# Last attention, first pass: one row maximum per bank of 500 columns instead of one over both banks

## The chip, the cores and the metric

One core of a Trainium2 chip runs the whole network in one launch. The metric is the device time of a launch in microseconds (us), the median of several runs. The engines of the core that matter here are PE (TensorE, matmul), DVE (VectorE), ACT (ScalarE), POOL (GpSimd) and SP (SyncE, which issues transfers). They run their own instruction streams in order and meet only at semaphores.

## What is computed

The network has four rounds of cross attention and feed-forward over 32 batches of 56 tokens; the keys and values come from a context of 1500 rows for each batch. The change lies in the last attention, cut here to what matters:

```python
def _L3_xattn_ref(query, key_value, Wq, bq, Wk, bk, Wv, bv, Wo, bo):
    NUM_HEADS = 16
    CLAMP = 10000.0
    ...
    scale = D ** (-0.5)
    q = (query @ Wq + bq).reshape(B, Nq, H, D).transpose(0, 2, 1, 3)
    k = (key_value @ Wk + bk).reshape(B, Nkv, H, D).transpose(0, 2, 1, 3)
    v = (key_value @ Wv + bv).reshape(B, Nkv, H, D).transpose(0, 2, 1, 3)
    attn = jnp.einsum('bhqd,bhkd->bhqk', q, k) * scale
    attn = jnp.clip(attn, -CLAMP, CLAMP)
    attn = jax.nn.softmax(attn, axis=-1)
    ...
    x = jnp.einsum('bhqk,bhkd->bqhd', attn, v).reshape(B, Nq, Cq)
    return x @ Wo + bo
```

With B = 32, Nq = 56, Nkv = 1500, 16 heads of 8 values. The softmax needs the maximum over the 1500 keys of each query and head before the exponential.

## The kernel before, in words

The function `clipped_pass` computes this attention in two passes over the scores of a batch. The first pass finds the maxima: with queries on the partitions (two heads of 56 queries, 112 rows) and keys on the free axis, 24 matmuls of 500 columns (eight pairs of heads, three thirds of the keys) are made two at a time. Such a pair of matmuls, each into a PSUM bank of its own, is a chunk; a batch has 12 chunks. `chunks` (PE) makes a chunk, `chunk_max` (DVE) takes the maximum of both banks in one reduction of 112 x 1000 elements to two columns of `mp`. After the twelfth, two small DVE instructions finish the eight maxima of the batch (`mu`, `mc`), POOL splits them into bf16 parts, and PE turns them.

The second pass makes the scores again, with keys on the partitions: 12 tiles of 125 keys, each 896 wide. For each tile PE scores it (`score`, 8 matmuls), DVE clips it out of PSUM (`clip_tile`), ACT takes the exponential, and PE multiplies it with the values (`weigh`, 16 small matmuls).

The two passes of different batches run interleaved. In slot k of batch b, PE makes in this order: the scores of tile k+2, the weighing of tile k, one chunk of the first pass of batch b+1 or b+2, and at last a piece of other work in the fifth bank (`fifth_bank`: the keys of batch b+3 in slots 0 to 2, the turning of the maxima, the sums, the values of the next batch in slots 7 to 10). DVE makes in the same slot: the clip of tile k+2, then the maximum of the chunk. The order is written out by hand; nothing is scheduled at run time.

Of the eight PSUM banks, 0 to 3 hold two score tiles, 4 the weighed sums, 5 the other work, and 6 and 7 the chunk (`CB[0]`). So the chunk has one buffer: PE's next chunk waits (`chunk_maxed`) until DVE's reduction of the last is done. Only the first 21 chunks, made before the second pass has begun, rotate over three pairs of banks (`CB[n % 3]`); the 363 chunks behind them (384 less 21) use banks 6 and 7 alone.

The keys made in the fifth bank are copied out by ACT twice (line 2119 as bf16, line 2123 in full), and PE's next keys wait for the second copy. In ACT's stream these two copies stand behind an exponential.

Of the kernel before, what the change touches and what calls it, by code (L numbers as in the profile page):

```python
# [19 lines left out]
ALU = mybir.AluOpType  # L20
ACT = mybir.ActivationFunctionType
AX = mybir.AxisListType
# [6 lines left out]
TT = 112  # L29
# [1598 lines left out]
def clipped_pass(core, L, S, src, bo, scale, clip, csum, ctx, norm):  # L1628

    nc, d, ps = core.nc, core.d, core.ps  # L1630

    def sb(n, shape, dt=F32, c=ctx):
        return core.sb(f"{L}_{n}", shape, dt, c)
# [13 lines left out]
    mp, mu, mc = sb("mp", [TT, 24]), sb("mu", [TT, 8]), sb("mc", [TT, 8])  # L1647
# [9 lines left out]
    CB = [slice(6, 8), slice(0, 2), slice(2, 4)]  # L1657
# [81 lines left out]
    first = Eight(None, 0)  # L1739
# [48 lines left out]
    with nc.Block() as block:  # L1788
        @block.sync
        def _(sp):  # L1790
            def place_part(b, n):
                sp.wait_ge((S["keys_first"], S["keys_second"], S["keys_third"])[n], b.lin(3, 3))
                for u, (part, _) in enumerate(PRODUCTS):
                    if part == n:
                        sp.dma_start(KS[b.r % 4][u:NPROD * PF:NPROD, 0:PAIRS * NK], key_part(b, part)[:, :]
                                     ).then_inc(S[f"keys_in{b.r % 4}"], 16)

            def place_keys(b):
                if b.turn is not None or b.r >= 4:
                    sp.wait_ge(S["scored"], b.lin(12, -36))  # L1800
                sp.wait_ge(S["keys_third"], b.lin(3, 3))
                for u, (part, _) in enumerate(PRODUCTS):
                    sp.dma_start(KS[b.r % 4][u:NPROD * PF:NPROD, 0:PAIRS * NK], key_part(b, part)[:, :]
                                 ).then_inc(S[f"keys_in{b.r % 4}"], 16)
# [122 lines left out]
        def _(pe):  # L1927
            def make_keys(b, c):
                if c == 0:
                    pe.wait_ge(S["ck_in"], b.lin(16, 16))  # L1930
                nc.tensor.matmul(key_bank(b, c), WK[:, :], CK[:, columns(c)], start=True, stop=True
                                 ).then_inc(S["keys_made"], 1)
# [59 lines left out]
            def chunks(b, c, pair=0):  # L1992

                if c == 0:
                    pe.wait_ge(S[f"keys_in{b.r % 4}"], uses(b, 4, 96))
                    pe.wait_ge(S[f"q_in{b.r % 4}"], uses(b, 4, 192) - (0 if b.r % 4 else 48))
                    if b.r == 0:
                        pe.wait_ge(S["q_first"], 48)
                if pair == 0 and (b.turn is not None or b.r >= 2 or (b.r, c) >= (1, 9)):
                    pe.wait_ge(S["chunk_maxed"], b.lin(12, c))  # L2000
                elif b.r or c >= 3:
                    pe.wait_ge(S["chunk_maxed"], b.lin(12, c - 2))
                for a in range(2):
                    m, p = (2 * c + a) // 3, (2 * c + a) % 3
                    mm = nc.tensor.matmul(ps[:, CB[pair].start + a, 0:500],  # L2005
                                          QS[b.r % 4][0:96, m * 2 * NQ:m * 2 * NQ + 128],
                                          KS[b.r % 4][0:96, m * NK + p * 500:m * NK + (p + 1) * 500],
                                          start=True, stop=True)
                mm.then_inc(S["chunk_scored"], 1)

            def uses(b, every, each):

                if b.turn is None:
                    return (b.r // every + 1) * each
                return (8 // every * each) * b.turn + (b.r // every + 1) * each

            def score(b, n):
                if n == 0:
                    pe.wait_ge(S["keys_zeroed"], min(2 * b.r + 2, 8))
                    pe.wait_ge(S[f"max_in{b.r % 2}"], uses(b, 2, 16))  # L2020
                if b.turn is not None or b.r or n >= 2:
                    pe.wait_ge(S["clipped"], b.lin(12, n - 1))
                for m in range(PAIRS):
                    k0 = m * NK + n * KP
                    mm = nc.tensor.matmul(SB[n % 2][:, m // 4, m % 4 * 2 * NQ:(m % 4 + 1) * 2 * NQ]  # L2025
                                          .rearrange("p (j q) -> p j q", j=2), KS[b.r % 4][:, k0:k0 + 128],
                                          queries(b)[:, m, :, :], start=True, stop=True)
                mm.then_inc(S["scored"], 1)
# [14 lines left out]
            def body(b):  # L2043
                for k in range(KT):
                    if k + 2 < KT:
                        score(b, k + 2)
                    elif (b + 1).there():
                        score(b + 1, k + 2 - KT)
                    weigh(b, k)
                    of, c = chunk_of(b, k)  # L2050
                    if of.there():
                        chunks(of, c)
                    fifth_bank(b, k)
# [28 lines left out]
            for n in range(21):  # L2082
                chunks(first + n // 12, n % 12, n % 3)
                if n == 13:
                    turn(first)
                if n in (16, 18, 20):
                    c = (n - 16) // 2
                    if c:
                        pe.wait_ge(S["keys_copied"], 6 + c)
                    else:  # L2090
                        pe.wait_ge(S["turn_copied"], 1)
                    make_keys(first + 2, c)
            pe.wait_ge(S["chunk_maxed"], 21)
            score(first, 0)
            score(first, 1)
            pe.wait_ge(S["ones_set"], 2)
# [129 lines left out]
        def _(dve):  # L2226
# [11 lines left out]
                         part_columns(P[:, 0:2, :], c))  # L2238
                dve.sem_inc(S["q_split"], 1)

            def chunk_max(b, c, pair=0):
                dve.wait_ge(S["chunk_scored"], b.lin(12, c + 1))
                nc.vector.tensor_reduce(mp[:, 2 * c:2 * c + 2], ps[0:TT, CB[pair], 0:500], AX.X, ALU.max  # L2243
                                        ).then_inc(S["chunk_maxed"], 1)
                if c < 11:
                    return
                dve.wait_ge(S["chunk_maxed"], b.lin(12, 12))
                nc.vector.tensor_reduce(mu[:, :], mp[:, :].rearrange("p (t c) -> p t c", c=3), AX.X, ALU.max
                                        ).then_inc(S["max_found"], 1)
                dve.wait_ge(S["max_found"], b.lin(1, 1))  # L2250
                nc.vector.tensor_scalar(mc[:, :], mu[:, :], clip, -clip, ALU.min, ALU.max
                                        ).then_inc(S["max_ready"], 1)

            def clip_tile(b, n):
                if n == 0:
                    dve.wait_ge(S[f"lb_in{b.r % 2}"], b_uses(b))
                dve.wait_ge(S["scored"], b.lin(12, n + 1))
                if b.turn is not None or b.r or n >= 3:
                    dve.wait_ge(S["weighed"], b.lin(12, n - 2))
                nc.vector.scalar_tensor_tensor(out=two(P[0:KP, n % 3, :]), in0=SB[n % 2][0:KP], scalar=0.0,  # L2260
                                               in1=two(LB[0:KP, b.r % 2, :]), op0=ALU.min, op1=ALU.max
                                               ).then_inc(S["clipped"], 1)
# [13 lines left out]
            def body(b):  # L2276
                for k in range(KT):
                    if k + 2 < KT:
                        clip_tile(b, k + 2)
                    elif (b + 1).there():  # L2280
                        clip_tile(b + 1, k + 2 - KT)
                    of, c = chunk_of(b, k)
                    if of.there():
                        chunk_max(of, c)
                    if b.r % 2 == 0 and (b - 2).there() and k == 3:
                        invert(b - 2)
# [16 lines left out]
            for t in VS:  # L2303
                nc.vector.memset(by_head(t)[:, :, DH:DH + 1], 1.0).then_inc(S["ones_set"], 1)
            for n in range(21):
                chunk_max(first + n // 12, n % 12, n % 3)
            clip_tile(first, 0)
            clip_tile(first, 1)
            batches(dve, body)
# [1508 lines left out]
```

## Time and profile before

| | us |
|---|---|
| median of 3 runs | 4166.52 |
| lowest and highest | 4165.03, 4169.4 |
| the profiled execution, device time | 4166.84 |
| its span in the trace | 4165.2 |
| of it, second pass with chunks beside it, about | 3264 to 4068 |

The last attention takes the stretch from about 3232 to 4105 us of the trace. The page's busy shares over the whole span (PE 87%, DVE 61%, ACT 50%, POOL 36%) are means over stages with different limits and do not tell what limits this one; in the slices of the page, DVE reads 9 tenths or more in the slices from 3330 us to 4060 us. The chain of work that ended last covers 1% of the span, so it cannot be used to follow this stage, and the stage is read by its own windows, waits and timeline.

### The profile page before, as it was taken

The numbers are of one execution on the slowest core, as the hardware profiler recorded it, in microseconds if no ns is written. First come the engines' busy times: TensorE is split into PE (matmuls) and PEld (weight loads), VectorE is DVE, ScalarE is ACT, GpSimd is POOL, SyncE is SP. The second block draws the span as 40 slices with busy tenths as digits, with TensorE's granted clock in tenths as the row PEclk, the third lists the DMA queues.
The fourth block names the chain that finished last, engine by engine and source line by source line (L and its number), as shares of the span: only waits on it lengthen the run. The fifth ranks groups of instructions, "written<-read, shape, count | busy, mean of one in ns | idle before, by whom it ended". The sixth has DMA issues, their size and how long they took to land. (4 is left out here: it accounts for less than half of the span.)

```text
span 4165.2 us, 84341 instructions
## 1 busy us (share of the span) xinstructions
PE 3629.1 (87%) x33160; PEld 2475.5 (59%) x33160; DVE 2526.5 (61%) x3567; ACT 2062.2 (50%) x2991; POOL 1478.7 (36%) x1913
## 2 busy tenths in 40 slices
PE   8499999937489999989999997589868799999987
PEld 8267777724466666656666664267633466666664
DVE  7556666544255554415545533567555899999994
ACT  8177777701134434434434342266412477777764
POOL 5275555131423323222332320022102666666640
PEclk9699999968689999989999997799978799999998
DMA  6177777546223323222323320111002666666650
GB/s 187 48 177 179 168 174 178 128 183 234 49 79 90 87 82 91 76 64 71 92 78 88 86 63 23 32 49 46 5 18 47 141 155 155 155 154 154 155 128 21
DMA packets 201964, 436.42 MB, mean 105 GB/s; under 512 B 46665, under 2 KB 103916, under 8 KB 201516
## 3 DMA queue, kind: packets, MB, share of 16 engines
q1 hardware_dynamic: 127196, 341.47, 31.5%
q0 software_dynamic: 38944, 47.04, 5.2%
q10 hardware_dynamic: 35504, 43.39, 3.8%
q8 instruction: 231, 3.78, 0.4%
q14 instruction: 89, 0.73, 0.1%
HBM read 246.72 MB, written 32.67 MB: 67 GB/s over the span
## 5 line engine op out<-in xcount | busy, mean ns | idle before, releaser
L1512 DVE TENSOR_REDUCE L_mp<-ps 128x2 f32<-128x1000 f32 (+1 forms) x352 | 402.5, 1152 | 562.0 <-PE ps L1310 558.5
L1347 PE MATMUL ps<-L_p,L_cn 125*97 125x448 f32 x1536 | 639.2, 538 | 0.0
L1494 ACT ACTIVATE L_p<-ps 125x896 f32<-125x896 f32 x384 | 352.0, 917 | 534.0 <-PE ps L1335 462.7
L2199 ACT ACTIVATE L_p<-L_p 125x896 f32<-125x896 f32 x384 | 364.5, 950 | 226.3 <-DVE L_p L2260 222.5
L2243 DVE TENSOR_REDUCE L_mp<-ps 112x2 f32<-112x1000 f32 x384 | 455.6, 1191 | 16.7 <-PE ps L2005 16.7
L2260 DVE SCALAR_TENSOR_TENSOR L_p<-ps,xn 125x896 f32<-125x896 f32 x384 | 414.3, 1081 | 17.0 <-PE ps L2025 16.7
L1333 PE MATMUL ps<-L_qh,L_ch 97*125 97x448 f32 x768 | 384.1, 500 | 0.0
L1347 PEld LDWEIGHTS ps<-L_p,L_cn 125*97 125x97 f32 x1536 | 250.4, 163 | 199.8 <-issue 165.9
L2005 PE MATMUL ps<-L_ks,L_qs 96*128 96x500 bf16 x768 | 236.3, 392 | 79.2 <-DVE L_mp L2243 65.9
L920 ACT ACTIVATE L_p<-ps,rk 125x896 f32<-125x896 f32 x256 | 257.5, 1007 | 50.7 <-PE ps L776 46.5
L1334 PE MATMUL ps<-L_ql,L_ch 96*125 96x448 f32 x768 | 282.3, 368 | 0.0
L1335 PE MATMUL ps<-L_qh,L_cl 96*125 96x448 f32 x768 | 280.8, 366 | 0.0
L1310 PE MATMUL ps<-L_cr,L_qb 96*128 96x500 f32 x672 | 234.8, 427 | 18.2 <-POOL L_qb L1235 18.0
L1780 POOL DMA_DIRECT2D L_qs<-L_q_part x381 | 211.7, 564 | 100.0 <-PE ps L2025 93.3
L2025 PEld LDWEIGHTS ps<-L_qs,L_ks 128*128 128x128 bf16 x3072 | 188.7, 98 | 75.5 <-issue 45.4
L776 PEld LDWEIGHTS ps<-L_qs,L_ks 128*128 128x128 bf16 x3072 | 188.1, 98 | 72.9 <-issue 54.9
L2038 PE MATMUL ps<-L_p,L_vs 125*18 125x112 f32 x6144 | 223.3, 263 | 2.5 <-ACT L_p L2199 2.1
L776 PE MATMUL ps<-L_qs,L_ks 128*128 128x112 bf16 x3072 | 216.1, 213 | 3.4 <-ACT L_p L920 3.4
L1260 POOL TENSOR_TENSOR L_un<-L_ue,L_rb 96x896 f32<-96x896 f32 x32 | 67.2, 2101 | 426.8 <-DMA L_rb<-L_den 426.8
L702 POOL DMA_DIRECT2D L_qs<-L_q_part x384 | 214.5, 567 | 7.6 <-DVEq L1042 6.8
L2025 PE MATMUL ps<-L_qs,L_ks 128*128 128x112 bf16 x3072 | 214.9, 213 | 2.6 <-DVE L_mp L2243 1.6
L692 POOL TENSOR_TENSOR L_k_part<-L_k_rest,L_k_part 128x500 bf16<-128x500 f32 x96 | 109.0, 1137 | 299.4 <-ACT L_k_part L885 299.3
(540 smaller groups left out, 7303.8 us busy)
## 6 DMA issues: line engine op xcount, KB each, us to landing
L_ks<-L_k_part SPq DMA_DIRECT2D x288, 375.0 KB, 6.0
L_ks<-L_k_first SPq DMA_DIRECT2D x96, 375.0 KB
moe_w<-in_L_w SPq DMA_DIRECT2D x64, 512.0 KB, 6.5
L_cn<-in_ctxN SPq DMA_DIRECT2D x32, 568.4 KB
cs_ct<-in_ctxT SPq DMA_DIRECT2D x32, 562.5 KB, 4.1
L_cr<-in_ctxT POOLq DMA_DIRECT2D x32, 562.5 KB
L_ch<-in_ctxT POOLq DMA_DIRECT2D x32, 562.5 KB, 4.5
L_raw<-in_ctxT SPq DMA_DIRECT2D x32, 562.5 KB, 5.0
```

Of the source, the lines that this page charges most:

```text
L776: mm = nc.tensor.matmul(SB[n % 2][:, m // 4, m % 4 * 2 * NQ:(m % 4 + 1) * 2 * NQ] .rearrange("p (j q) -> p j q", j=2), KS[b.r % 3][:, k0:k ...
L920: nc.scalar.activation(weights_at[n % 3][0:KP, :].rearrange("p (a n) -> p a n", a=2), SB[n % 2][0:KP], ACT.Exp, scale=rk[:, b.lin(KT, n):b ...
L1333: nc.tensor.matmul(SB[n % 2][:, a, :], CH[s][:, k], QH[s][:, q], start=True, stop=False)
L1334: nc.tensor.matmul(SB[n % 2][:, a, :], CH[s][0:DC, k], QL[s][:, q], start=False, stop=False)
L1335: mm = nc.tensor.matmul(SB[n % 2][:, a, :], CL[s][:, k], QH[s][0:DC, q], start=False, stop=True)
L1347: mm = nc.tensor.matmul(U[:, a, :], CN[s][:, j, :], P[:, n % 2, a * HALF:(a + 1) * HALF], start=(j == 0), stop=(j == KT - 1))
L1494: nc.scalar.activation(two(P[:, n % 2, :]), SB[n % 2], ACT.Exp).then_inc(S["exped"].sem, 1)
L1512: nc.vector.tensor_reduce(mp[:, 2 * k:2 * k + n], ps[:, bank:bank + n, 0:500], AX.X, ALU.max).then_inc(S["chunk_maxed"].sem, 1)
L2025: mm = nc.tensor.matmul(SB[n % 2][:, m // 4, m % 4 * 2 * NQ:(m % 4 + 1) * 2 * NQ] .rearrange("p (j q) -> p j q", j=2), KS[b.r % 4][:, k0:k ...
L2199: nc.scalar.activation(two(P[0:KP, n % 3, :]), two(P[0:KP, n % 3, :]), ACT.Exp).then_inc(S["exped"], 1)
L2243: nc.vector.tensor_reduce(mp[:, 2 * c:2 * c + 2], ps[0:TT, CB[pair], 0:500], AX.X, ALU.max).then_inc(S["chunk_maxed"], 1)
L2260: nc.vector.scalar_tensor_tensor(out=two(P[0:KP, n % 3, :]), in0=SB[n % 2][0:KP], scalar=0.0, in1=two(LB[0:KP, b.r % 2, :]), op0=ALU.min, ...
```

## The change

A chunk behind the first 21 is reduced by two instructions of 112 x 500, one for each bank, in place of one of 112 x 1000. The signals count banks instead of chunks: each of the two matmuls raises `chunk_scored`, each reduction raises `chunk_maxed`. DVE waits for the first matmul before the first reduction and for the second before the second. PE waits before each matmul for the reduction that last read its bank, so that the first matmul of the next chunk may start when the first of the two reductions is done. The first 21 chunks keep one reduction, which raises the count by two. No instruction changes its place in any engine's stream; 363 DVE instructions are added.

```diff
-                if pair == 0 and (b.turn is not None or b.r >= 2 or (b.r, c) >= (1, 9)):
-                    pe.wait_ge(S["chunk_maxed"], b.lin(12, c))
-                elif b.r or c >= 3:
-                    pe.wait_ge(S["chunk_maxed"], b.lin(12, c - 2))
+                ahead = b.r == 0 or (b.r == 1 and c < 9)
+                if ahead and (b.r or c >= 3):
+                    pe.wait_ge(S["chunk_maxed"], 2 * b.lin(12, c - 2))
                 for a in range(2):
+                    if not ahead:
+                        pe.wait_ge(S["chunk_maxed"], b.lin(24, 2 * c + a - 1))
                     m, p = (2 * c + a) // 3, (2 * c + a) % 3
-                    mm = nc.tensor.matmul(ps[:, CB[pair].start + a, 0:500],
+                    nc.tensor.matmul(ps[:, CB[pair].start + a, 0:500],
                                           QS[b.r % 4][0:96, m * 2 * NQ:m * 2 * NQ + 128],
                                           KS[b.r % 4][0:96, m * NK + p * 500:m * NK + (p + 1) * 500],
-                                          start=True, stop=True)
-                mm.then_inc(S["chunk_scored"], 1)
+                                          start=True, stop=True).then_inc(S["chunk_scored"], 1)
...
-            def chunk_max(b, c, pair=0):
-                dve.wait_ge(S["chunk_scored"], b.lin(12, c + 1))
-                nc.vector.tensor_reduce(mp[:, 2 * c:2 * c + 2], ps[0:TT, CB[pair], 0:500], AX.X, ALU.max
-                                        ).then_inc(S["chunk_maxed"], 1)
+            def chunk_max(b, c, pair=0, ahead=False):
+                if ahead:
+                    dve.wait_ge(S["chunk_scored"], b.lin(24, 2 * c + 2))
+                    nc.vector.tensor_reduce(mp[:, 2 * c:2 * c + 2], ps[0:TT, CB[pair], 0:500], AX.X, ALU.max
+                                            ).then_inc(S["chunk_maxed"], 2)
+                else:
+                    for a in range(2):
+                        dve.wait_ge(S["chunk_scored"], b.lin(24, 2 * c + a + 1))
+                        nc.vector.tensor_reduce(mp[:, 2 * c + a:2 * c + a + 1], ps[0:TT, CB[0].start + a, 0:500],
+                                                AX.X, ALU.max).then_inc(S["chunk_maxed"], 1)
                 if c < 11:
                     return
-                dve.wait_ge(S["chunk_maxed"], b.lin(12, 12))
+                dve.wait_ge(S["chunk_maxed"], b.lin(24, 24))
...
             for n in range(21):
-                chunk_max(first + n // 12, n % 12, n % 3)
+                chunk_max(first + n // 12, n % 12, n % 3, True)
```

## Rows read from the trace of the kernel before

**Rows 1.** Busy time by stretch: us and instructions per engine, PE's granted clock, DMA.
```profile
3300.00:4060.00 760.00, 695.57 (x10217) 465.47 (x10215) 749.13 (x770) 538.03 (x862) 448.45 (x762) 1.00 0.67 151
```

**Rows 2.** DVE's groups, 3300 to 4060 us: busy us, mean ns | idle before them.
```profile
L2243 DVE TENSOR_REDUCE L_mp<-ps 112x2 f32<-112x1000 f32 x349 | 415.5, 1191 | 0.0
L2260 DVE SCALAR_TENSOR_TENSOR L_p<-ps,xn 125x896 f32<-125x896 f32 x349 | 377.0, 1080 | 8.9 <-PE ps L2025 8.9
```

**Rows 3.** Waits, 3300 to 4060 us: total us, times, longest us.
```profile
ACT L_p L2199 <- DVE L_p L2260: 204.8, 306, 1.6
PEld ps L2005 <- DVE L_mp L2243: 123.9, 279, 0.9
...
PE ps L2005 <- DVE L_mp L2243: 62.8, 134, 0.7
...
DVE L_p L2260 <- PE ps L2025: 8.9, 28, 0.3
```

**Rows 4.** Timeline, two slots with values in bank five: start us, us, engine, line.
```profile
3607.35 1.19 DVE L2243 TENSOR_REDUCE L_mp<-ps 112x2 f32<-112x1000 f32 x1
...
3608.45 1.08 DVE L2260 SCALAR_TENSOR_TENSOR L_p<-ps,xn 125x896 f32<-125x896 f32 x1
...
3608.59 0.11 PEld L2005 LDWEIGHTS ps<-L_ks,L_qs 96*128 96x128 bf16 x2 [0.20 <-DVE L_mp L2243]
3608.59 0.60 PE L2005 MATMUL ps<-L_ks,L_qs 96*128 96x500 bf16 x2
...
3609.03 0.82 PE L1938 MATMUL ps<-L_wve,L_cv 97*125 97x128 f32 x6
3609.45 1.19 DVE L2243 TENSOR_REDUCE L_mp<-ps 112x2 f32<-112x1000 f32 x1
...
3609.69 0.56 PE L2025 MATMUL ps<-L_qs,L_ks 128*128 128x112 bf16 x8
...
3610.18 0.58 PE L2038 MATMUL ps<-L_p,L_vs 125*18 125x112 f32 x16
...
3610.56 1.08 DVE L2260 SCALAR_TENSOR_TENSOR L_p<-ps,xn 125x896 f32<-125x896 f32 x1
...
3610.70 0.60 PE L2005 MATMUL ps<-L_ks,L_qs 96*128 96x500 bf16 x2
```

**Rows 5.** Timeline of DVE before the second pass: twelve 1000-wide maxima back to back.
```profile
3235.50 13.37 DVE L2243 TENSOR_REDUCE L_mp<-ps 112x2 f32<-112x1000 f32 x12 [3.71 <-PE ps L2005]
```

**Rows 6.** Timeline of DVE in the first attention: 500-wide reductions out of PSUM.
```profile
701.18 0.67 DVE L969 TENSOR_REDUCE img_most<-ps 128x1 f32<-128x500 f32 x1
701.77 0.67 DVE L970 TENSOR_REDUCE img_least<-ps 128x1 f32<-128x500 f32 x1
702.35 0.25 DVE L977 RECIPROCAL L_rc<-ps 112x16 f32<-112x16 f32 x1
```

**Rows 7.** Timeline of all engines in two slots with keys in bank five.
```profile
3590.64 1.08 DVE L2260 SCALAR_TENSOR_TENSOR L_p<-ps,xn 125x896 f32<-125x896 f32 x1
...
3591.76 0.95 ACT L2199 ACTIVATE L_p<-L_p 125x896 f32<-125x896 f32 x1 [1.16 <-DVE L_p L2260]
...
3593.08 0.58 ACT L2123 ACTIVATE L_k_full<-ps 128x500 f32<-128x500 f32 x1
...
3593.71 1.10 PE L1931 MATMUL ps<-L_ck,L_wk 97*128 97x500 f32 x2
...
3594.65 0.56 PE L2025 MATMUL ps<-L_qs,L_ks 128*128 128x112 bf16 x8
...
3595.25 1.09 DVE L2260 SCALAR_TENSOR_TENSOR L_p<-ps,xn 125x896 f32<-125x896 f32 x1 [0.32 <-PE ps L2025]
```

**Rows 8.** Timeline of DVE where the second pass starts, with its idle times.
```profile
3284.22 1.20 DVE L2243 TENSOR_REDUCE L_mp<-ps 112x2 f32<-112x1000 f32 x1 [5.91 <-PE ps L2005]
...
3286.79 1.20 DVE L2243 TENSOR_REDUCE L_mp<-ps 112x2 f32<-112x1000 f32 x1 [0.38 <-PE ps L2005]
```

More of the change, by code:

```diff
@@ L2092, in _ @@
                     make_keys(first + 2, c)
-            pe.wait_ge(S["chunk_maxed"], 21)
+            pe.wait_ge(S["chunk_maxed"], 42)
             score(first, 0)
```

## The prediction

> **What bounds the kernel now.** I first took the busy time by stretch, because the page's shares are means over four attentions and four feed-forwards. From 3300 to 4060 us of the trace DVE is busy 749.1 of 760 us, 98.6%; PE has 695.6 us (91.5%), ACT and POOL far less, and PE's granted clock is full [rows 1]. Next the groups of DVE in that stretch: 349 maxima of 1000 columns and 349 clips of 896 columns are nearly all of its work, with 8.9 us of idle time in front of the clips and none in front of the maxima [rows 2]. Then the waits: PE stands 124 us at its weight loads and 63 us at its matmuls for the maximum of the chunk before, but DVE stands only 8.9 us for PE, 28 times 0.3 us [rows 3]. The big waits are on engines that have time; the small one is on the engine that has none. So DVE sets the pace, and what this stage costs is the number of slots times what DVE issues in one.
>
> The timeline shows the slot. From one maximum to the next are 2.10 us: 1.10 us from the start of the maximum to that of the clip, 1.00 us from the clip to the maximum [rows 4]. These are less than the recorded durations of 1.19 and 1.08 us, because the records of neighbours overlap by some 0.09 us; so instructions of DVE must be priced by the distance of their starts, not by their lengths. PE's chunk starts 0.05 us behind the end of the maximum (3607.35 + 1.19 = 3608.54, start 3608.59) and lasts 0.60 us, so it is there at about 3609.19, and DVE, still in the clip, comes to its maximum only at 3609.45 [rows 4]. DVE never waits for the chunk: a chunk that is made earlier gives DVE nothing.
>
> **The change part by part.**
>
> *The split of the maximum, on the path.* Before: twelve maxima back to back take 13.37 us, so (13.37 - 1.19) / 11 = 1.107 us each [rows 5], the same as the 1.10 and 1.11 us to the clip in the slots [rows 4]. After: two reductions of 500 columns. This form, out of PSUM, float32 and to one column, stands in the first attention as a pair, 96 times: 701.18 to 701.77 to 702.35, 1.17 us for the two [rows 6]. The split thus costs 1.17 - 1.106 = 0.064 us a chunk. The price is not zero, since a 1000-wide one of 1.106 us and a 500-wide one of 0.585 us leave 0.521 us for the other 500 columns and 0.064 us that every instruction pays. There are 384 - 21 = 363 split chunks: 363 x 0.064 = 23.2 us. The rows resolve 0.01 us, so the bounds are 1.16 - 1.11 = 0.05 us and 1.18 - 1.10 = 0.08 us, 18.2 and 29.0 us in all. A far bound is the difference of the recorded lengths, 2 x 0.665 - 1.191 = 0.139 us (0.67 us in [rows 6], 1191 ns in [rows 2]), which would hold only if the two did not overlap. I take the middle one: the form, the memory and the overlap are those of the row.
>
> A page speaks to this price. The Trainium skill, Perfetto Trace Analysis, section Optimizing Scalar/DVE Operations, puts the access overhead of a DVE instruction on PSUM at about 125 ns and advises larger operations where the engine is saturated. By it the sum of this part would be 363 x 0.125 = 45 us in place of 23; the rows show half of it, 0.064 us. The same section holds that breaking up instructions may pay where an engine is not saturated but makes others wait; the 98.6% above is the condition that fails here.
>
> *The waits and signals added on DVE.* Each half waits for its own matmul. Both matmuls are done some 0.26 us before the first half comes up, by the working above, so no wait ends there. A satisfied wait and an increment cost nothing to be seen: the maxima of [rows 5] carry both and still stand 1.107 us apart. Nothing is added; what would be if that cover went is 0.2 us or more a slot, but the clip of 1.00 us in front stays.
>
> *PE's waits, off the path.* The first matmul of a chunk may now start at the end of the first half, some 0.58 us earlier, the second where the chunk started before. Queued behind the second are the fifth bank's work, the next scores and the weighing. The chunk's two matmuls take 0.44 us of PE's issue (3608.59 to 3609.03), so the work behind it can come up to 0.22 us earlier, where PE was waiting. PE needs 0.44 + 0.66 + 0.49 + 0.52 = 2.11 us in a slot with values (the differences of the starts in [rows 4]); DVE's new slot is 2.10 + 0.064 = 2.165 us, so there PE keeps 0.05 us to spare, and in slots without values more. PE does not become the bound.
>
> *The 28 stalls.* What could be given back is the DVE idle time of 8.9 us [rows 3]. It lies in one slot of each batch, the one behind the second keys: the clip that would start 2 x 2.10 = 4.20 us after that of 3590.64 starts 4.61 us after it, at 3595.25 [rows 7], a stall of 0.41 us (0.32 of it recorded as idle). The chain to it is: clip at 3590.64, exponential at 3591.76, the two copies of the keys behind it in ACT's stream, the second from 3593.08 to 3593.66, PE's next keys at 3593.71, the scores at 3594.65, done at 3595.21, the clip [rows 7]. No maximum and no chunk is a link of this chain, so an earlier bank does not shorten it; it stays 4.61 us. But DVE's own two slots in it grow from 4.20 to 4.33 us, and this growth is hidden in the stall: 28 x 2 x 0.064 = 3.6 us not paid.
>
> *Where the pass starts.* Up to 3287 us DVE stands idle, 5.91 us at the longest, for chunks whose operands come late [rows 8]; about five split maxima lie in front of such a gap and cost nothing: 0.3 us not paid. The same gaps wait on transfers and not on free banks, so nothing is won there.
>
> Sum: 23.2 - 3.6 - 0.3 = +19.3 us. On the profiled execution, 4166.84 us of device time (span 4165.2 and 1.6 us around it), this makes 4186.1 us. The median of the runs is 0.3 us under the profiled one, 4166.52, and gives 4185.8. I forecast 4186 us, 0.46% slower.
>
> **The rivals.**
>
> *The stalls go away.* If the second keys in fact come late because PE came late out of its chunk, PE's lead of 0.22 us and the longer slots take the stall out. Then 28 x 0.41 = 11.5 us are won and no growth is hidden: 23.2 - 11.5 - 0.3 = +11.4, 4178 us. For it speaks that PE did wait for the maximum just before (the waits of [rows 3] are as frequent as four slots in five); against it the chain of [rows 7], in which PE's keys start 0.05 us after ACT's copy.
>
> *The dearer split.* If the overlap of the records is lost between two reductions that wait on one semaphore, the price is 0.139 us: 363 x 0.139 = 50.5, less 28 x 0.28 = 7.8 hidden and 0.7, +42, 4209 us. Against it: [rows 5], the same instruction with the same wait, overlapped. By the 125 ns of the Trainium skill's page, an estimate, the same working gives 45.4 - 7.0 - 0.6 = +38, 4205 us, and the rows do not bear that out.
>
> *The other side: not slower.* The mechanism is that a free bank half a maximum earlier does take the stalls, and that the second half costs less than on [rows 6], because it is the same operation on the next bank. It decides where 363 times the price equals 11.5 us plus 0.3, at 0.033 us a chunk. At 0.02 us: 7.3 - 11.8 = -4.5, 4162 us. With the low bound of 0.05 us and the stalls gone it is still 18.2 - 11.8 = +6.4, 4173 us. Everything needed for a gain over 0.2% speaks against rows; there is just not more than 11.5 us of idle time to be had.
>
> *The change does not do what it says.* PE's second matmul might be held by its own wait so that the chunk ends where it did, or later by its weight load (0.11 us for the two weight loads, [rows 4]). This would cost PE alone, which has time in all slots but those with keys and values, and leaves DVE's price: again about 4186 us. It is not told apart by the time, only by PE's waits.
>
> **How the numbers follow.** A measurement of this kernel can tell about 0.2% from no change, 8.3 us: slower begins at 4174.9, faster at 4158.2. Forecast 0.74 (4181 to 4191 by the bounds of 0.05 and 0.08 us: 18.2 - 2.8 - 0.3 = +15.1 and 29.0 - 4.5 - 0.4 = +24.1); stalls gone 0.11; dearer split 0.07; other side and the low bound with the stalls gone 0.08. The range reaches down over the second case, to 4175, and up to 4195, which takes in the high bound of the price and a little of what lies between it and the dearer split. Slower 0.89, same 0.08, faster 0.03.
>
> **What would show each step.** In the changed trace the reductions read 112x1 out of 112x500, about 0.66 us long, with starts 0.58 to 0.59 us apart and the same from the second half to the clip. The slot is 2.16 to 2.17 us. From clip to clip over the two key slots it is still 4.61 us, and the idle time of DVE in front of the clips falls from 8.9 us to about 28 x 0.19 = 5.4 us, not to zero. PE's waits for the maximum before its chunk stay in sum over 100 us, since DVE got slower. The distance from the first to the last split maximum grows by 19 us, and no other stage changes. I am wrong if DVE's share of the stretch falls under 98%, if the halves stand 0.6 us or more apart, or if the 28 waits are gone.

## The result, and the profile after

The changed kernel takes 4186.46 us (median of 5 runs, 4182.34 to 4189.58), the kernel before in the same runs 4166.52 us (4163.31 to 4169.84). The ratio is 1.0044, with a 95% interval of 1.0031 to 1.0058: slower by 0.44%, where 0.46% and 4186 us were forecast. That the median meets the forecast to 0.5 us is luck: the five runs of each kernel spread over 6.5 to 7.2 us. The ratios here and below are of runs at nearly the same granted clock; one of the four runs of the quarters (4359.43 us, clock 0.857 where the others have 0.927 and 0.928) is left aside.

First the busy time of the changed kernel from 3300 to 4060 us, the line that answers to [rows 1] (columns: stretch, its length, PE, PE's weight loads, DVE, ACT, POOL, each with instructions, then PE's granted clock, DMA share, GB/s):

```profile
3300.00:4060.00 760.00, 709.65 (x9997) 460.80 (x9996) 752.79 (x1094) 529.40 (x849) 452.43 (x759) 1.00 0.67 152
```

DVE has gone from 749.1 to 752.8 of 760 us, and PE's matmuls in the same 760 us from 10217 to 9997: DVE is fuller and less gets done. PE's busy time rises all the same, from 695.6 to 709.7 us, but this is no more work: two matmuls of a chunk that run together are recorded with 0.60 us for both, two that stand apart with 0.38 us each. DVE's groups, which answer to [rows 2] (busy us, mean ns | idle before):

```profile
L2249 DVE TENSOR_REDUCE L_mp<-ps 112x1 f32<-112x500 f32 x683 | 425.8, 661 | 0.0
L2266 DVE SCALAR_TENSOR_TENSOR L_p<-ps,xn 125x896 f32<-125x896 f32 x341 | 366.2, 1074 | 5.3 <-PE ps L2025 5.3
```

And the waits, as [rows 3] (total us, times, longest us):

```profile
PEld ps L2006 <- DVE L_mp L2249: 112.5, 276, 0.5
...
PE ps L2006 <- DVE L_mp L2249: 41.6, 173, 0.3
...
DVE L_p L2266 <- PE ps L2025: 5.3, 28, 0.2
```

PE's waits for the maximum did what the change is made for: at the matmuls from 62.8 to 41.6 us, at the weight loads from 123.9 to 112.5. DVE's 28 idle times are still 28, and their sum is 5.3 us (forecast: 5.4). The timeline shows the slot and the chain of [rows 7] again, here in the changed kernel (start us, us):

```profile
3602.62 0.38 PE L2006 MATMUL ps<-L_ks,L_qs 96*128 96x500 bf16 x1 [0.29 <-DVE L_mp L2249]
3603.07 1.07 DVE L2266 SCALAR_TENSOR_TENSOR L_p<-ps,xn 125x896 f32<-125x896 f32 x1
...
3603.20 0.38 PE L2006 MATMUL ps<-L_ks,L_qs 96*128 96x500 bf16 x1 [0.20 <-DVE L_mp L2249]
...
3604.07 1.24 DVE L2249 TENSOR_REDUCE L_mp<-ps 112x1 f32<-112x500 f32 x2
3604.18 0.95 ACT L2199 ACTIVATE L_p<-L_p 125x896 f32<-125x896 f32 x1 [1.22 <-DVE L_p L2266]
...
3605.24 1.07 DVE L2266 SCALAR_TENSOR_TENSOR L_p<-ps,xn 125x896 f32<-125x896 f32 x1
...
3605.50 0.58 ACT L2123 ACTIVATE L_k_full<-ps 128x500 f32<-128x500 f32 x1
3606.13 1.11 PE L1931 MATMUL ps<-L_ck,L_wk 97*128 97x500 f32 x2 [0.27 <-ACT L_k_full L2123]
3606.24 1.24 DVE L2249 TENSOR_REDUCE L_mp<-ps 112x1 f32<-112x500 f32 x2
...
3607.67 1.09 DVE L2266 SCALAR_TENSOR_TENSOR L_p<-ps,xn 125x896 f32<-125x896 f32 x1 [0.19 <-PE ps L2025]
...
3608.08 0.60 PE L2006 MATMUL ps<-L_ks,L_qs 96*128 96x500 bf16 x2
...
3608.68 1.25 DVE L2249 TENSOR_REDUCE L_mp<-ps 112x1 f32<-112x500 f32 x2
```

In this slot PE's two matmuls of the chunk are 0.58 us apart, each released by its own half (3602.62, 3603.20). So it is in some quarter of the chunks; in most of the others PE comes to the chunk later and makes both together (3608.08). DVE's pair of halves goes from 3604.07 to the clip at 3605.24: 1.17 us, where [rows 4] has 1.10. The chain through ACT is what it was, from the clip at 3603.07 to that at 3607.67: 4.60 us against 4.61 before.

Where the time went can be read from the first maximum and from the small instruction that closes the maxima of a batch (`mc`, line 2251 before, 2257 after). First the kernel before (the first maximum is [rows 5]), its third and its last `mc`:

```profile
3309.73 0.17 DVE L2251 TENSOR_SCALAR L_mc<-L_mu 112x8 f32<-112x8 f32 x1
...
4068.20 0.17 DVE L2251 TENSOR_SCALAR L_mc<-L_mu 112x8 f32<-112x8 f32 x1
```

and the changed kernel, its first maxima and the same two:

```profile
3240.14 13.36 DVE L2244 TENSOR_REDUCE L_mp<-ps 112x2 f32<-112x1000 f32 x12 [4.17 <-PE ps L2006]
...
3315.77 0.17 DVE L2257 TENSOR_SCALAR L_mc<-L_mu 112x8 f32<-112x8 f32 x1
...
4091.46 0.17 DVE L2257 TENSOR_SCALAR L_mc<-L_mu 112x8 f32<-112x8 f32 x1
```

From the first maximum to the last `mc` the kernel before takes 4068.20 - 3235.50 = 832.7 us, the changed one 4091.46 - 3240.14 = 851.3 us: +18.6 us, where 19.3 were forecast. The two profiled executions differ by 22.0 us (4188.88 less 4166.84); the other 3.4 us lie outside the stage, +4.6 ahead of its first maximum, in code that is the same, and -1.2 behind it, in work that the change does not touch. From the third to the last `mc` lie 29 batches, and this distance serves below as a measure free of what other stages do: 758.5 us before, 775.7 us after, 26.15 and 26.75 us a batch (+17.2 us). From the first maximum to the third `mc` it is 74.2 us before and 75.6 after, +1.4.

### The profile page after: what moved, and what is told of

Same layout as the page of the kernel before. It is cut to its first block and busy times, and to the rows that moved or that the text cites. A ratio compares the mean times of both kernels' runs of the same rounds, so it can differ in the third digit from the quotient of the medians.

```text
span 4187.3 us, 84725 instructions
## 1 busy us (share of the span) xinstructions
PE 3664.1 (88%) x33160; PEld 2486.1 (59%) x33160; DVE 2548.1 (61%) x3930; ACT 2063.1 (49%) x2991; POOL 1479.3 (35%) x1913
## 5 line engine op out<-in xcount | busy, mean ns | idle before, releaser
L2249 DVE TENSOR_REDUCE L_mp<-ps 112x1 f32<-112x500 f32 x726 | 452.6, 662 | 8.3 <-PE ps L2006 8.3
L2006 PE MATMUL ps<-L_ks,L_qs 96*128 96x500 bf16 x768 | 263.0, 396 | 60.4 <-DVE L_mp L2249 45.8
```

What stands on the lines that cost most here:

```text
L2006: nc.tensor.matmul(ps[:, CB[pair].start + a, 0:500], QS[b.r % 4][0:96, m * 2 * NQ:m * 2 * NQ + 128], KS[b.r % 4][0:96, m * NK + p * 500:m ...
L2249: nc.vector.tensor_reduce(mp[:, 2 * c + a:2 * c + a + 1], ps[0:TT, CB[0].start + a, 0:500], AX.X, ALU.max).then_inc(S["chunk_maxed"], 1)
```

## The experiments

The theory: DVE sets the pace of the stage, each added reduction costs 0.064 us of it, the bank freed early gives DVE nothing, and the one stall that DVE has is set by the copies of the keys in ACT. The rivals: the price hangs on the waits and signals; the early bank gives something back; the stall is PE's lateness out of the chunk. "29 batches" is the distance just described. On their chips the kernel before took 4171.4 us (first four) and 4168.1 us (last two), so the ratios are compared, not the microseconds. The distance within a trace can be compared across them: a slot without keys has on average 2.10 us from clip to clip in the kernel before, in the signals only and in the key bank freed first, and 2.17 us in the change, in the split only and in the two edits together, this last on the other chip.

| | ratio to before | 95% interval | third and last `mc`, us | 29 batches, us | against before |
|---|---|---|---|---|---|
| before | 1 | | 3309.73, 4068.20 | 758.5 | |
| the change | 1.0044 | 1.0031 to 1.0058 | 3315.77, 4091.46 | 775.7 | +17.2 |
| split only | 1.0042 | 1.0027 to 1.0058 | 3316.67, 4093.71 | 777.0 | +18.6 |
| signals only | 1.0005 | 0.9995 to 1.0014 | 3317.16, 4077.44 | 760.3 | +1.8 |
| quarters | 1.0138 | 1.0119 to 1.0156 | 3320.92, 4135.56 | 814.6 | +56.2 |
| key bank freed first | 0.9977 | 0.9968 to 0.9986 | 3312.66, 4062.03 | 749.4 | -9.1 |
| the same, with the change | 1.0023 | 1.0013 to 1.0033 | 3307.63, 4075.94 | 768.3 | +9.8 |
| one bank's maximum only | 0.9840 | 0.9820 to 0.9860 | 3308.07, 3998.22 | 690.2 | -68.3 |

### The split alone

```diff
-                nc.vector.tensor_reduce(mp[:, 2 * c:2 * c + 2], ps[0:TT, CB[pair], 0:500], AX.X, ALU.max
-                                        ).then_inc(S["chunk_maxed"], 1)
+                    for a in range(2):
+                        last = nc.vector.tensor_reduce(mp[:, 2 * c + a:2 * c + a + 1],
+                                                       ps[0:TT, CB[0].start + a, 0:500], AX.X, ALU.max)
+                    last.then_inc(S["chunk_maxed"], 1)
```

> The DVE half of the change alone: two reductions of 112x500 for each of the 363 chunks, but one wait for both matmuls before them, one signal behind the second, and PE's next chunk waits for both banks as in the kernel before. The theory (DVE sets the pace, each added instruction costs 0.064 us, the bank freed early gives DVE nothing): 4186 us, as with the whole change, +19.3 us over the kernel before; starts of the halves 0.58 to 0.59 us apart; 28 DVE idle times of 0.19 us in front of the clip behind the second keys. The rival that the early bank gives back part of the stalls: without it they stay at 0.3 us each and the time is 3 to 6 us above the whole change, 4189 to 4192 us. The rival that part of the price is the second wait and signal: under 4186 us, down to the kernel before.

The ratio is 1.0042 against 1.0044: all of the price is there without any of the new waits. In the 29 batches it is 1.3 us slower than the whole change, 777.0 against 775.7. So the change's waits by bank give back 0.05 us a batch and no more. The 28 idle times are what they were:

```profile
PEld ps L2005 <- DVE L_mp L2248: 138.8, 284, 1.0
PE ps L2005 <- DVE L_mp L2248: 69.1, 127, 0.8
...
DVE L_p L2266 <- PE ps L2025: 5.3, 28, 0.2
```

The last line is the same, 5.3 us, as in the whole change, though PE waits 138.8 and 69.1 us in place of 112.5 and 41.6. Some 54 us of PE's waiting are taken away by the early bank, and DVE's 28 idle times do not change by them.

### The signals alone

```diff
-                    for a in range(2):
-                        dve.wait_ge(S["chunk_scored"], b.lin(24, 2 * c + a + 1))
-                        nc.vector.tensor_reduce(mp[:, 2 * c + a:2 * c + a + 1], ps[0:TT, CB[0].start + a, 0:500],
-                                                AX.X, ALU.max).then_inc(S["chunk_maxed"], 1)
+                    dve.wait_ge(S["chunk_scored"], b.lin(24, 2 * c + 2))
+                    nc.vector.tensor_reduce(mp[:, 2 * c:2 * c + 2], ps[0:TT, CB[0], 0:500], AX.X, ALU.max
+                                            ).then_inc(S["chunk_maxed"], 2)
```

(The diff is against the changed kernel.)

> The signals of the change alone: PE waits before each of a chunk's two matmuls and signals behind each, DVE makes one reduction of 112x1000 that waits for both and raises the count by two. The theory (all of the price is the added DVE instruction): no change from the kernel before, 4166.5 us within 0.1%. The rival that waits and signals per bank cost something on PE or DVE: up to 4186 us; a wait that held each second matmul by its weight load of 0.06 us would show as chunks of over 0.60 us on PE and still cost nothing, since PE has time.

No difference that the times can tell, 1.0005. The trace is finer: the 29 batches take 1.8 us more. These lie in one slot of each batch, the one behind the stall, which the forecast had not looked at; the other eleven slots are as long as before, to 0.005 us on average. In the kernel before:

```profile
3595.25 1.09 DVE L2260 SCALAR_TENSOR_TENSOR L_p<-ps,xn 125x896 f32<-125x896 f32 x1 [0.32 <-PE ps L2025]
...
3595.65 0.60 PE L2005 MATMUL ps<-L_ks,L_qs 96*128 96x500 bf16 x2
...
3596.29 1.20 DVE L2243 TENSOR_REDUCE L_mp<-ps 112x2 f32<-112x1000 f32 x1
```

and in the kernel with the signals alone:

```profile
3603.34 1.09 DVE L2265 SCALAR_TENSOR_TENSOR L_p<-ps,xn 125x896 f32<-125x896 f32 x1 [0.29 <-PE ps L2025]
...
3603.74 0.60 PE L2006 MATMUL ps<-L_ks,L_qs 96*128 96x500 bf16 x2
...
3604.45 1.20 DVE L2248 TENSOR_REDUCE L_mp<-ps 112x2 f32<-112x1000 f32 x1
```

Here PE is late, and the chunk ends (3595.65 + 0.60 = 3596.25) only 0.04 us before the maximum starts. That start is 1.04 us behind the clip's and not 1.00: DVE does wait for the chunk, in this one slot. With a wait in front of each matmul and a signal behind each it starts 0.11 us behind the chunk's end (3603.74 + 0.60 = 3604.34, start 3604.45), 1.11 us behind the clip. The 0.07 us once a batch are 2 us over the stage. In the changed kernel the first half needs only the first matmul, and the distance is 1.01 us (3607.67 to 3608.68). That is most of the 0.05 us a batch by which the change is faster than the split alone, where it is 1.04 again:

```profile
3609.08 1.09 DVE L2266 SCALAR_TENSOR_TENSOR L_p<-ps,xn 125x896 f32<-125x896 f32 x1 [0.19 <-PE ps L2025]
3610.12 1.26 DVE L2248 TENSOR_REDUCE L_mp<-ps 112x1 f32<-112x500 f32 x2
```

### Quarters

```diff
-                        nc.vector.tensor_reduce(mp[:, 2 * c + a:2 * c + a + 1], ps[0:TT, CB[0].start + a, 0:500],
-                                                AX.X, ALU.max).then_inc(S["chunk_maxed"], 1)
+                        for h in range(2):
+                            last = nc.vector.tensor_reduce(mp[:, 4 * c + 2 * a + h:4 * c + 2 * a + h + 1],
+                                                           ps[0:TT, CB[0].start + a, 250 * h:250 * h + 250],
+                                                           AX.X, ALU.max)
+                        last.then_inc(S["chunk_maxed"], 1)
```

> The changed kernel with two reductions of 112x250 for each bank, so four for each chunk, with waits and signals by bank as in the change; the last small reduction reads 48 columns in place of 24 (32 times some 0.025 us). The theory (a fixed 0.064 us for each instruction, 0.26 us for 250 columns): starts 0.32 us apart, slot 2.30 us; 363 x 0.192 = 69.7 us, plus 0.8 us for the small reductions, less 28 x 0.384 = 10.8 us that the stall behind the second keys hides and less 0.9 us at the start: +58.8, 4225 us, and the stalls shrink to 0.02 us. The rival that the price hangs on waits and signals: 4186 us as with the change, since these are as many. The rival that instructions this short no longer overlap: 0.07 us more each, over 4270 us.

1.0138 is +57.5 us on 4166.5, where +58.8 were expected, with the waits and signals of the change. The timeline of DVE:

```profile
3591.00 1.38 DVE L2251 TENSOR_REDUCE L_mp<-ps 112x1 f32<-112x250 f32 x4
3592.30 1.08 DVE L2270 SCALAR_TENSOR_TENSOR L_p<-ps,xn 125x896 f32<-125x896 f32 x1
3593.30 1.38 DVE L2251 TENSOR_REDUCE L_mp<-ps 112x1 f32<-112x250 f32 x4
```

Four quarters take from 3591.00 to the clip at 3592.30, 1.30 us, 0.325 each; a half takes 0.585 and a whole chunk 1.106. The steps are 0.26 and 0.52 us for 250 and 500 columns, and what is left is the same 0.065 us each time. The slot is 2.30 us, and DVE's idle time in front of the clips has left the list of waits: the two slots of 4.60 us fill the chain of 4.61.

### The key bank freed first

```diff
-                nc.scalar.activation(key_part(b, 0)[:, columns(c)], key_bank(b, c), ACT.Copy
-                                     ).then_inc(S["keys_first"], 1)
...
                 nc.scalar.activation(Kf[:, columns(c)], key_bank(b, c), ACT.Copy).then_inc(S["keys_copied"], 1)
+                act.wait_ge(S["keys_copied"], b.lin(3, c + 1))
+                nc.scalar.activation(key_part(b, 0)[:, columns(c)], Kf[:, columns(c)], ACT.Copy
+                                     ).then_inc(S["keys_first"], 1)
...
-                pool.wait_ge(S["keys_copied"], b.lin(3, c + 1))
+                pool.wait_ge(S["keys_first"], b.lin(3, c + 1))
```

> The kernel before, with ACT's two copies of the keys turned round: the full copy is taken out of the bank first and frees it for PE's next keys; the bf16 copy is then made from the full one in SBUF, and POOL, which overwrites that, waits for it. PE's work and its places are the same, the link in ACT is some 0.47 us shorter. The theory (the stall behind the second keys is set by the chain clip, exponential, two copies, next keys, scores, clip of 4.61 us): the chain falls to 4.14 us, under DVE's 4.20, the 28 stalls vanish, and 28 x 0.41 = 11.5 us are won: 4155 us. The rival that PE's late chunk, held by the maximum, makes the stall: the stalls stay and the time is 4166 us.

0.9977: faster than both kernels, by 9.6 us on 4166.5, and no idle time of DVE is left in the stretch. So the chain through ACT was the cause of the stall, and no freer chunk bank is needed to remove it. But 11.5 us were expected; the times cannot tell the two apart (the interval is 6 to 13 us), the 29 batches can. The timeline of this kernel in the slots with keys shows what is late next:

```profile
3590.34 0.60 PE L2005 MATMUL ps<-L_ks,L_qs 96*128 96x500 bf16 x2 [0.60 <-DVE L_mp L2244]
...
3592.18 0.57 ACT L2121 ACTIVATE L_k_full<-ps 128x500 f32<-128x500 f32 x1
3592.31 1.08 DVE L2261 SCALAR_TENSOR_TENSOR L_p<-ps,xn 125x896 f32<-125x896 f32 x1
...
3592.62 0.60 PE L2005 MATMUL ps<-L_ks,L_qs 96*128 96x500 bf16 x2
...
3593.05 1.00 PE L1931 MATMUL ps<-L_ck,L_wk 97*128 97x500 f32 x2
...
3593.89 0.56 PE L2025 MATMUL ps<-L_qs,L_ks 128*128 128x112 bf16 x8
...
3594.49 1.09 DVE L2261 SCALAR_TENSOR_TENSOR L_p<-ps,xn 125x896 f32<-125x896 f32 x1
```

PE's keys at 3593.05 follow its chunk at once, not a copy; ACT's first copy had ended at 3592.75. But PE's own slots with keys are 2.28 us (3590.34 to 3592.62), longer than DVE's 2.10, and two in a row make the scores end at 3594.45, so the clip comes 2.18 us behind the last and not 2.10. A residue of 0.08 us and the 0.04 us of the late chunk remain of 0.41 + 0.04 us: some 0.33 us a batch can be won, and 9.1 us over the 27 batches with keys in this distance are 0.34.

### The same with the change

The two edits together.

> The changed kernel (split maxima, waits by bank) with ACT's copies of the keys turned round as in the experiment on the kernel before. The theory: only 0.28 us of each stall was left, so 28 x 0.28 = 7.8 us are won, 4178.6 us, and against the kernel before with the same turn the split now costs its full 23 us, as nothing of it is hidden. The rival in which the stall is PE's lateness: no gain, 4186 us.

In the 29 batches it is 775.7 - 768.3 = 7.4 us faster than the change, as expected (7.8). The second half of the expectation was a little off: against the kernel before with the same turn the split costs 768.3 - 749.4 = 18.9 us in 348 chunks, 0.054 us each and not 0.064. The difference, some 0.12 us a batch, fits the residue of 0.08 us and the 0.04 us of the late chunk just described, which the longer slots of DVE and the waits by bank take away.

### One bank's maximum only

```diff
-                    for a in range(2):
-                        dve.wait_ge(S["chunk_scored"], b.lin(24, 2 * c + a + 1))
-                        nc.vector.tensor_reduce(mp[:, 2 * c + a:2 * c + a + 1], ps[0:TT, CB[0].start + a, 0:500],
-                                                AX.X, ALU.max).then_inc(S["chunk_maxed"], 1)
+                    dve.wait_ge(S["chunk_scored"], b.lin(24, 2 * c + 2))
+                    nc.vector.tensor_reduce(mp[:, 2 * c:2 * c + 1], ps[0:TT, CB[0].start, 0:500], AX.X, ALU.max
+                                            ).then_inc(S["chunk_maxed"], 2)
```

> The changed kernel with the second reduction of each of the 363 chunks left out: the maximum is taken over the first bank only, so half of the first pass's maxima is not computed; the first waits for both matmuls and frees both banks. It measures what the stage takes when DVE has time. The theory: DVE's own slot falls from 2.165 to 1.58 us, and PE takes over with what it issues, some 23.5 to 24.5 us a batch against 26.2 before: 4100 to 4125 us. If something else than DVE held the slots at 2.1 us, the time would stay over 4155 us.

0.984, 4099 us (two runs); this kernel leaves out half of the maxima and only measures what the stage takes when DVE has time. The stage falls to 690.2 / 29 = 23.8 us a batch, and the busy time of this kernel shows who has taken over (columns as above, stretch from 3300 to 3990 us), with its waits below:

```profile
3300.00:3990.00 690.00, 685.21 (x10173) 462.91 (x10165) 606.36 (x767) 528.96 (x858) 448.78 (x762) 1.00 0.74 166
```

```profile
DVE L_p L2265 <- PE ps L2025: 73.6, 186, 0.8
...
PEld ps L2006 <- DVE L_mp L2248: 22.2, 105, 0.3
```

PE is busy 685 of 690 us, and now DVE waits 73.6 us for it. Taking 0.585 us of DVE out of each of 363 slots, 212 us in all, gained 87 us on the changed kernel and no more, since PE takes over at 23.8 us a batch, 2.4 us below the pace of before. These 2.4 of 26.15 us, some 9% of the stage, are also about the most that relief of DVE alone can bring while PE's work stays as it is.

## Why the prediction was right

**The bound.** DVE at 98.6%, priced by the distance of starts. The last experiment confirms it from the other side: with DVE relieved the stage follows PE.

**The price of the split.** 0.064 us from the first attention's 500-wide reductions ([rows 6]) and the back-to-back maxima ([rows 5]). Measured: 1.17 us for two halves against 1.106, and the quarters give 0.065 as well. The recorded lengths, 0.661 against 1.191 us, would have said 0.13 us, close to the 0.139 us that the prediction turns into 4209 us; the records of neighbours overlap, and that overlap does not cost DVE time. The 125 ns of the Trainium skill's page (Perfetto Trace Analysis, section Optimizing Scalar/DVE Operations) are not borne out by this kernel: 0.064 us in halves, 0.065 in quarters. Its advice, larger operations where the engine is saturated, is.

**The waits and signals.** Priced at nothing; measured 1.8 us in the signals-only trace, within the noise of the times. This is a real miss in the working, small and turned round in the changed kernel: the text said that DVE never waits for the chunk, read from a slot with values. In the slot behind the stall it does, by 0.04 us, and there the change gives back 0.03 us a batch, 0.05 us with all that the waits by bank bring. "A chunk that is made earlier gives DVE nothing" is thus wrong by 1.3 us over the stage.

**The sum.** Over the 29 batches the prediction's terms give 348 x 0.064 = 22.3 us less 27 x 0.128 = 3.5 us hidden, 18.8 us. The split alone measured 18.6 us, the whole change 17.2, the difference being the 1.3 us given back. From the first maximum to the third `mc` the terms give 15 x 0.064 - 0.13 - 0.3 = 0.5 us, and 1.4 us were measured. The changed kernel behind the long gap of [rows 8]:

```profile
3288.96 1.26 DVE L2249 TENSOR_REDUCE L_mp<-ps 112x1 f32<-112x500 f32 x2 [5.76 <-PE ps L2006]
...
3291.54 1.26 DVE L2249 TENSOR_REDUCE L_mp<-ps 112x1 f32<-112x500 f32 x2 [0.32 <-PE ps L2006]
3293.08 1.09 DVE L2266 SCALAR_TENSOR_TENSOR L_p<-ps,xn 125x896 f32<-125x896 f32 x1 [0.27 <-PE ps L2025]
3294.47 1.26 DVE L2249 TENSOR_REDUCE L_mp<-ps 112x1 f32<-112x500 f32 x2 [0.30 <-PE ps L2006]
```

The split maxima in front of the gap cost nothing, as forecast: to the maximum behind it are 3284.22 - 3235.50 = 48.7 us before and 3288.96 - 3240.14 = 48.8 after (there are three of them, not five). But behind it DVE waits for PE three more times, where the kernel before waits once more, 0.38 us [rows 8]; the prediction has no term for this. The 1.6 us too much over the 29 batches and the 0.9 us too little at the start have opposite signs, and that the stage's 18.6 us come within 0.7 us of 19.3 owes something to it.

**The stall.** The chain of 4.61 us was read right: 4.60 after the change, idle time 5.3 us against a forecast of 5.4. The first rival, that PE's lead removes it, was wrong: PE's waits fell by 54 us against the split alone and the idle time did not move, and turning round two copies in ACT removed it with PE's waits as they were. What the working with 0.41 us a stall missed, in the rival and in the expectation of the run, is the next in line, PE's own 2.28 us slots with keys: they keep 0.08 us a batch, and the late chunk behind them 0.04 us.

**The other rivals.** The dearer split and the other side needed prices of 0.139 and under 0.033 us; the price is 0.064.

## What to carry to other kernels

Before an instruction is cut in two to free its buffer earlier, look at which engine waits. Here PE's waits for the maximum, 63 us at its matmuls and 124 us at its weight loads, were among the largest numbers of the stage and worth 1.3 us; DVE's 9 us counted; and each added instruction on the full engine cost its fixed share, save for the few that a stall hid. Price instructions of a full engine by the distance between their starts, from the nearest shape that the trace has. And follow a stall's chain link by link: the remedy was not at the buffer with the long waits but at the order of two copies on a third engine.

## What the runs showed of the hardware that was not expected

With a wait in front of each of two back-to-back matmuls and a signal behind each, in place of one wait and one signal for both, the waiting engine started 0.11 us behind their recorded end instead of 0.04 us (signals-only against before, one slot in each batch). Which of these is the cause was not tried apart: it may be the second signal, the wait in front of the second matmul, or the end of the matmuls, which is modelled in the trace. It was seen only where the consumer was waiting for the very matmul.
